# Splitting the opening loads of a fused attention and FFN kernel over two issuing queues and shortening the first layer-norm roots

## The reference

```
xn = layernorm(x)                        # no gain or offset, eps 1e-5
q, k, v = xn @ wq, xn @ wk, xn @ wv      # 32 query heads, 8 key/value heads of 128
q, k = rope(q), rope(k)
s = softmax(mask(q k^T / sqrt(128))) v @ wo      # causal, sliding window of 128
W1, W3, W2 = dequant_q40(...)            # 4-bit weights, one scale per 64
g = silu( (silu(xn @ W1^T) * (xn @ W3^T)) @ W2^T )
out = x + s * g
```

## Time and profile before

| | |
|---|---|
| median of 3 executions | 802.93 us (802.49 to 803.28) |
| the profiled execution's own time | 802.51 us |
| its span, from the first to the last instruction | 800.7 us |
| TensorE busy | 796.0 us (99%), 3966 matmul instructions |
| VectorE, ScalarE, GpSimd busy | 567.6, 428.9, 475.4 us |
| granted TensorE clock over the span | 1.00 |

### The profile page before, as it was taken

One profiled execution on the slowest core, in us unless ns is written; L12 is line 12 of the kernel. 1 busy time (PEld: TensorE's weight loads), 2 busy tenths in 40 slices (PEclk: granted clock), 3 DMA queues, 4 the chain that ended last, 5 costly groups with the idle time before them and its releaser, 6 DMA issues.

```text
span 800.7 us, 13470 instructions
## 1 busy us (share of the span) xinstructions
PE 796.0 (99%) x3966; PEld 671.8 (84%) x3966; DVE 567.6 (71%) x1636; ACT 428.9 (54%) x1104; POOL 475.4 (59%) x357
## 2 busy tenths in 40 slices
PE   9999999999999999999999999999999999999998
PEld 7888888888888888888888888888888888888887
DVE  7725867667448867777786777778677777867785
ACT  5413313223138675666666565666656566665672
POOL 2103314224256774867487486748757674878997
PEclk9999999999999999999999999999999999999999
DMA  9659425201000400400040040004004000420102
GB/s 273 192 180 271 135 71 158 78 28 53 2 27 14 132 14 1 132 2 14 2 131 13 0 131 0 13 0 131 13 0 130 1 13 0 131 65 0 40 1 106
DMA packets 51909, 54.00 MB, mean 67 GB/s; under 512 B 4129, under 2 KB 33185, under 8 KB 51873
## 3 DMA queue, kind: packets, MB, share of 16 engines
q1 hardware_dynamic: 51728, 53.50, 22.2%
q10 hardware_dynamic: 144, 0.07, 0.0%
HBM read 47.25 MB, written 6.29 MB: 67 GB/s over the span
## 4 chain that ended last, share of the span: by engine, by line
PE 92%; POOL 4%; issue 2%; DMA 1%; ACT 0%; SPq 0%; DVE 0%; POOLq 0%; ACTq 0%
PE bank L1332 26%; PE bank L1333 26%; PE bank L1334 26%; PE bank L1523 3%; PE bank L1539 3%; PE bank L1556 2%; PE bank L1557 2%; PE bank L1558 2%; PE bank L1565 1%; POOL swap L453 1%; PE bank L1562 1%; PE bank L1563 1%; DMA raw<-in_wv 1%; POOL acc L484 1%; POOL q L457 1%
## 5 line engine op out<-in xcount | busy, mean ns | idle before, releaser
L453 POOL TENSOR_TENSOR swap<-swap,cst 128x512 f32<-128x512 f32 x80 | 108.1, 1351 | 41.7 <-ACT swap L697 41.7
L718 ACT ACTIVATE probs<-probs,nmx 128x128 f32<-128x128 f32 x256 | 100.0, 392 | 59.7 <-DVE nmx L1106 59.7
L1332 PE MATMUL bank<-xh,wih 128*128 128x512 f32 x320 | 128.9, 403 | 0.0
L1333 PE MATMUL bank<-xl,wih 128*128 128x512 f32 x320 | 125.2, 391 | 0.0
L1334 PE MATMUL bank<-xh,wil 128*128 128x512 f32 x320 | 125.0, 391 | 0.0
L1332 PE MATMUL bank<-woh,oh 128*128 128x512 f32 (+1 forms) x260 | 100.8, 388 | 0.0
L1333 PE MATMUL bank<-wol,oh 128*128 128x512 f32 (+1 forms) x260 | 100.6, 387 | 0.0
L1334 PE MATMUL bank<-woh,ol 128*128 128x512 f32 (+1 forms) x260 | 100.5, 387 | 0.0
L401 POOL TENSOR_TENSOR hl<-act_h,hh 128x512 fp32r<-128x512 f32 x22 | 31.6, 1436 | 99.5 <-ACT hh L599 99.5
L457 POOL TENSOR_TENSOR q<-q,swap 128x512 f32<-128x512 f32 x64 | 86.0, 1344 | 6.6 <-DVE q L1081 1.6
L476 POOL TENSOR_TENSOR ph<-ph,cst 128x512 fp32r<-128x512 f32 x32 | 41.9, 1309 | 73.2 <-ACT ph L733 73.2
(11 more groups left out here) (139 smaller groups left out, 2025.8 us busy)
## 6 DMA issues: line engine op xcount, KB each, us to landing
raw<-in_wq SPq DMA_DIRECT2D x32, 256.0 KB, 4.7
raw<-in_wo SPq DMA_DIRECT2D x32, 256.0 KB, 4.8
pk<-in_w SPq DMA_DIRECT2D x44, 128.0 KB, 3.6
sc<-in_s SPq DMA_DIRECT2D x44, 128.0 KB, 3.7
vals<-stage SPq DMA_DIRECT2D x16, 256.0 KB, 2.9
vraw<-vals SPq DMA_DIRECT2D x16, 256.0 KB, 2.9
pk<-in_w SPq DMA_DIRECT2D x11, 256.0 KB, 2.6
sc<-in_s SPq DMA_DIRECT2D x11, 256.0 KB, 3.0
```

The source lines that it names most:

```text
L453: nc.gpsimd.tensor_tensor(v, v, spread(sin.unsqueeze(1), P, 2, SEQ), ALU.mult).then_inc(sin_done, 1)
L718: e = nc.scalar.activation(probs[:, s, c0:c1], probs[:, s, c0:c1], ACT.Exp, bias=nmx[:, s, i:i + 1], scale=-1.0, accum_out=rsum[:, s, i:i ...
L1332: nc.tensor.matmul(out_, sh, mh, start=(i == 0), stop=False)
L1333: nc.tensor.matmul(out_, sh, ml, start=False, stop=False)
```

## The change

- The load of x tile 0 is cut into two transfers of 64 rows. Rows 0 to 63 are issued by SP on the old semaphore, rows 64 to 127 by ACT on a new one, `x_rest`. `stats(0)` waits for both.
- The load of wv block (0,0) moves from SP's list to ACT's, behind that half tile. The identity's load follows it. All three stand ahead of ACT's wait for the memset and ahead of its first square root.
- In SP's list x tiles 2 and 3 move ahead of wv blocks (1,2) and (1,3).
- In `scales` the factor -0.5 is folded into the operation that adds eps. Tiles 0 and 1 are then refined in two operations, the first of which multiplies r by r, taken as a per-partition scalar, and by v; tiles 2 to 7 keep three, the second now a plain product. `LN_AT` and one wait count change with it.

```diff
-        LN_AT = (0, 5, 10, 16)
+        LN_AT = (0, 4, 8, 14)
...
-            load_x(0)
-            load_wv(0, 0)
+            sp.dma_start(xn[0:HALF, 0, :], x_v[0:HALF, 0, :]).then_inc(x_in[0], 16)
             load_wv(0, 1)
             load_wv(0, 2)
             load_x(1)
             load_wv(0, 3)
-            for d in range(DT):
-                load_wv(1, d)
-            for i in range(2, NT):
+            load_wv(1, 0)
+            load_wv(1, 1)
+            load_x(2)
+            load_x(3)
+            load_wv(1, 2)
+            load_wv(1, 3)
+            for i in range(4, NT):
                 load_x(i)
...
+            act.dma_start(xn[HALF:P, 0, :], x_v[HALF:P, 0, :]).then_inc(x_rest, 16)
+            act.dma_start(raw[:, 0, :], wv[0:P, 0:VH]).then_inc(raw_in[0], 16)
+            act.dma_start(ident, const[:, C_ID:C_ID + P]).then_inc(id_in, 16)
             act.wait_ge(warm_set, 2)
             nc.scalar.activation(warm[:, 1:2], warm[:, 0:1], ACT.Sqrt)
-            act.dma_start(ident, const[:, C_ID:C_ID + P]).then_inc(id_in, 16)
...
                 dve.wait_ge(x_in[i], 16)
+                if i == 0:
+                    dve.wait_ge(x_rest, 16)
...
-                nc.vector.tensor_scalar(v, mv[:, first:last, 1], EPS, None, ALU.add).then_inc(ln_small, 1)
+                nc.vector.tensor_scalar(v, mv[:, first:last, 1], EPS, -0.5, ALU.add, ALU.mult).then_inc(ln_small, 1)
                 dve.wait_ge(std_done, part + 1)
                 nc.vector.reciprocal(r, r0).then_inc(ln_small, 1)
                 dve.wait_ge(ln_small, LN_AT[part] + 2)
-                nc.vector.tensor_tensor(t, r, r, ALU.mult).then_inc(ln_small, 1)
-                dve.wait_ge(ln_small, LN_AT[part] + 3)
-                nc.vector.scalar_tensor_tensor(out=r0, in0=t, scalar=-0.5, in1=v, op0=ALU.mult,
-                                               op1=ALU.mult).then_inc(ln_small, 1)
-                dve.wait_ge(ln_small, LN_AT[part] + 4)
+                if len(tiles) == 1:
+                    nc.vector.scalar_tensor_tensor(out=r0, in0=r, scalar=r, in1=v, op0=ALU.mult,
+                                                   op1=ALU.mult).then_inc(ln_small, 1)
+                    dve.wait_ge(ln_small, LN_AT[part] + 3)
+                else:
+                    nc.vector.tensor_tensor(t, r, r, ALU.mult).then_inc(ln_small, 1)
+                    dve.wait_ge(ln_small, LN_AT[part] + 3)
+                    nc.vector.tensor_tensor(r0, t, v, ALU.mult).then_inc(ln_small, 1)
+                    dve.wait_ge(ln_small, LN_AT[part] + 4)
                 nc.vector.scalar_tensor_tensor(out=t, in0=r0, scalar=1.5, in1=r, op0=ALU.add,
...
             def two_norms(i):
-                dve.wait_ge(ln_small, LN_AT[i] + 5)
+                dve.wait_ge(ln_small, LN_AT[i] + 4)
```

More of the change, by code:

```diff
@@ L146, in build @@
         x_in = [sem(f"x_in{i}") for i in range(NT)]
+        x_rest = sem("x_rest")
         w13_in = [[sem(f"w13_in{i}{m}") for m in range(2)] for i in range(2)]
```

## The result

The changed kernel took 804.90 us (median of 9 executions, 803.66 to 806.46) against 802.51 us for the kernel before (9 executions). The ratio is 1.0028, with a 95% interval of 1.0019 to 1.0036: slower by about 2.2 us, outside the forecast range of 801.8 to 803.4 and on the wrong side. The profiled execution took 805.29 us, its span 803.5 us, 2.8 more than the span before.

The account below looks back on a forecast made before the run. TensorE is full after 19 us, so only the opening counts: of 0.52 won on the norm chain block (1,1)'s arrival passes 0.15; with 0.08 that is 0.23, say 0.3, giving 802.6 us, range 801.8 to 803.4.

Parts of the forecast that it names:

- What bounds the kernel: Whole kernel: TensorE is full from 19 to 780 us, so the change can only win or lose time before 19 us.
- The three issues on ACT: Opening, ACT's queue: issues of about 0.47 each, identity issued at 1.69, landing at 4.5 or at worst 6.3; cost zero.
- The bound of 4.6 us: Identity's load on ACT: worst-case time to landing, taken from tile 1 in SP's crowded queue, giving a landing at 6.3.
- Block (0,0) at "zero": Opening, ScalarE: wants the block at 4.7; it was issued at the same time before, so moving it costs zero.
- The end of the range: Total time: upper limit of the forecast range, 803.4 us, leaving out part of the slower rivals.
- No case gets past 1.6: TensorE's opening: at most 1.2 us to win, so over 0.2% (1.6 us) faster or slower got 0.03 each.
- Rival 3: ACT's queue delivers late, delaying tile 0's half; loss once over 0.39 late; 1.0 late gives 803.5; chance 0.10.
- The split: Load of tile 0 on two queues: lands 0.15 us earlier, bounds 0 and 0.34.
- The root: Layer norms of tiles 0 and 1: one refinement operation removed, 0.20 us less per tile; tiles 2 to 7 zero.
- the scalar operand: Remaining refinement operation in the root: per-partition scalar instead of a constant, taken as zero, bounded at 0 to 0.10.
- Tiles 2 and 3: SP's list: moved ahead of blocks (1,2) and (1,3), gains nothing itself; the blocks' later arrival costs zero.
- The table load: ACT's opening: moves behind the three issues, ending at 3.44; 0.4 us of cover before the first root, so zero.

Follow-up runs that it names:

- e7: Changed kernel with 25 matmuls on zeros in place of 12 ahead of the first transposes, same loads; 805.54 us, ratio 1.0033 to the kernel before.
- e10: Changed kernel with 18 matmuls on zeros in place of 12, same loads; 804.02 us, ratio 1.0017 to the kernel before.
- e6: Changed kernel with tile 0 in one piece; ACT issues tile 0, block (0,0) and the identity, SP starts with block (0,1); 803.72 us.
- e13: Changed kernel with tile 0 cut into two column halves instead of row halves, on the same two queues; 803.57 us, ratio 1.0009 to the kernel before.
- e1: Changed kernel with the identity's load first of ACT's three; 804.29 us, ratio 1.0018 to the kernel before.
- e9: Changed kernel with the identity second and block (0,0) third on ACT's queue; 805.90 us, ratio 1.0041 to the kernel before.
- e12: Changed kernel, but SP issues its half tile and block (0,1), then waits until the identity has landed; 806.38 us, ratio 1.0044 to the kernel before.
- e2: Changed kernel with block (0,0) back on SP behind its half tile; ACT issues the other half, then the identity; 803.09 us, ratio 1.0002 to before.
- e4: Changed kernel with tile 0 whole on SP; ACT issues block (0,0), then the identity; 803.04 us, ratio 1.0002 to the kernel before.
- e5: Changed kernel with both row halves of tile 0 and block (0,0) on SP; ACT issues the identity alone; 803.55 us, ratio 1.0011 to before.
- e14: Edit of e5: both halves of tile 0 on SP, cut by columns in place of rows; 803.84 us, ratio 1.0015 to the kernel before.
- e3: Kernel before with the shorter root alone, loads and queues unchanged; 802.62 us, ratio 1.0000 to the kernel before.
- e8: Kernel before with the shorter root and x tiles 2 and 3 ahead of blocks (1,2) and (1,3), queues unchanged; 802.57 us, ratio 0.9998.
- e11: Kernel before with the shorter root, x tiles 2 and 3 moved ahead, and 10 matmuls on zeros in place of 12; 802.63 us, ratio 0.9999.

## Why the prediction was wrong

**What bounds the kernel: held.** The stretch behind 19 us is full in both, and all of the loss is in the opening.

**The three issues on ACT: this step failed.** It bounded the identity's landing at 6.3 and took the cost as zero. The identity landed at 8.6, and in the two other profiles with the same loads at 7.3 and 7.2 (e7, e10), against a need of TensorE at 5.84. The wrong premise was that a transfer's landing follows from its place in its own queue. What stands third on ACT's queue beside SP's list came at 7.2 or later in all seven profiles in which SP's list ran freely: the identity at 8.6, 7.7, 7.3, 7.2 and 7.9 (changed, e6, e7, e10, e13), block (0,0) at 7.7 and 7.3 (e1, e9). What stands second came anywhere from 4.5 to 7.8. With SP held back the third came at 5.8 (e12), and with only two loads on ACT the identity came at 4.1 and 6.4 (e2, e4) and the time was that of before. The identity went from ahead of nearly everything to behind 384 KB of its own queue. The issues also took 0.58, 0.86 and 0.45 and not 0.47 each, so it was issued at 2.25 instead of 1.69. The bound of 4.6 us came from an early transfer of SP's crowded queue; the largest of the rows beside it, 6.6, would have given 8.3.

**Block (0,0) at "zero" failed too, but not in every execution.** It took 6.4 us from issue to landing in the changed kernel's profile and landed at 7.8; in e7 and e10 it landed at 4.6, when ScalarE wanted it. Before it was the first behind tile 0 in the only busy queue, 1.20 to 4.35. How often it is late in the changed kernel is not known: one execution of it was profiled, at 805.29 among the slower of the nine.

**The end of the range failed with it.** "No case gets past 1.6" counted only what could be won. On the side of loss a late input has no such end, and TensorE's stop carries a price that was not in the sum: some 0.9 us by e10 for the clock. What is left, some 1.3 us, is by the timeline the late start itself, less the waits for weight blocks that it swallows; no run parts these two.

**Rival 3 had the right place and the wrong piece.** It saw ACT's queue deliver late, but hung it on the half tile. That landed at 3.9, 0.4 later than the whole tile before, at the 0.39 from which it had worked out a loss; the loads behind it decided.

**The split: 0.15 predicted, nothing found.** Where ACT's half stood first, tile 0 was complete at 3.7 to 4.0 in place of 3.6 (changed, e2, e7, e9, e10, e12). The Trainium skill, page "DMA: Bandwidth & Descriptors", section "Rules for kernel authors", gives 0 for this term, and the runs agree that nothing is won. With both halves on SP the kernel was slower than before (e5, ratio 1.0011; e14, 1.0015). The section "Issuing engines are not separate DMA queues" of the same page of the Trainium skill says that transfers of different issuers interleave on the same engines. The trace agrees (e4: side by side, tile 0 at 4.2 in place of 3.6), and here that was a loss and not only a missing gain.

**The root: right in kind, 0.13 instead of 0.20 per tile**, the bounded 0.06 of the scalar operand being real. As forecast the end of the kernel sees none of it (e3: 1.0000). **Tiles 2 and 3: right**, zero (e8: 0.9998). **The table load: right**: it ended at 4.01, and the root of tile 0, at 4.97, waited for VectorE.

**What stays open.** Most profiles have a stretch with a low transfer rate between 3 and 6 us, deeper or shallower (the mean of these 3 us goes from 167 to 381 GB/s); neither the shape of the halves nor the number of queues explains it alone. With SP's as the only busy queue, block (1,1) landed at anything from 10.0 to 11.2, with the same loads ahead of it (before, e3, e8, e11). How the 2.2 us split between the row shape and the two queues is known only roughly, from e13 (803.57) and e2 (803.09), since the clock's fall can amplify small differences. Why one list of loads lands block (0,0) at 4.6 in two profiles and at 7.8 in a third is not known.

## What to carry to other kernels

Moving a load to a second issuing queue gives it no engines of its own; it lets the loads of both queues run side by side, and the first needed one arrives later (e4). Order the opening's loads by when they are needed, across all queues together. The small one that gates the busiest engine (here 64 KB of identity) was there by 3.8 wherever it led its queue; but nothing else that is needed first may then stand behind it, as the half tile did in e1. No order tried here beat that of before. Before moving a load, ask what its landing would be if everything issued until then went ahead of it: here 1 MB, which the kernel before had in at 6.6 us (block (0,2)), an estimate past the bound of 6.3 and nearer to the 7.2 to 8.6 measured. Ask too what the stop costs TensorE in clock as well as in time.

## What the runs showed that was not expected

- A load of 64 rows x 2 KB took 0.57 to 0.58 us to issue, one of 128 rows x 2 KB 0.39 to 0.41 and one of 128 rows x 1 KB 0.39 to 0.41 at the same moment (changed, e4, e6, e13): half the bytes for nearly half as much again.
- TensorE stood still for 2.98 us, from 5.7 to 8.7, and its granted clock fell from 2.4 to 1.2 GHz within that stop, just after 8.0; it was back by 11.5. Stops of 2.62 and 2.19 us (profiles of e1 and e13) brought the same fall, in e13 only after work had been taken up again at 7.96. With stops of 0.54 (e10), 1.27 (e6) and 1.63 us (e9's profile) it did not fall.
- The matmuls on zeros changed from 0.21 to 0.11 us a step at 5.0 in the profile of before, at 4.7 in the changed kernel's, and not before their last, at 6.1, in e3's.
